# Wave attention: low parts of x on VectorE, sine tables from one rounded angle per phase, projection products ordered by part

## The reference, cut to what matters

```
qkvg = x @ Wqkvg.T + bqkvg                 # 256 -> 1024 channels
q_feat, k_feat = elu(q) + 1, elu(k) + 1
deposit = k_feat * v
alpha, omega, phi = softplus(wave_damping), wave_frequency, wave_phase
kernels = exp(-alpha * t) * cos(omega * t + phi)      # t = 0 .. 511, 16 heads
kernels /= sum(abs(kernels))
convolved = causal convolution of deposit with kernels (512 places)
field_c = softmax(field_coupling) @ convolved         # over heads
out = (q_feat * field_c * sigmoid(gate)) @ Wout.T + bout
x = layernorm(x + out)
```

## Time and profile before

| | |
|---|---|
| time, median of 3 | 1128.72 us |
| profiled execution, first to last instruction | 1136.1 us |
| PE busy | 1029.5 us (91%) |
| DVE busy | 792.9 us (70%) |
| ACT busy | 461.3 us (41%) |
| POOL busy | 467.0 us (41%) |
| wave attention | about the first 173 us of the span |

### The profile page before, as it was taken

The page is one execution under the profiler, slowest core; times in us unless marked ns, Lnnn a source line. Parts: engine busy times, 40 slices in busy tenths (PEclk is TensorE's granted clock), DMA queues, the critical chain, the costliest instruction groups (busy, mean ns, idle before and its releaser), DMA issues.

```text
span 1136.1 us, 19209 instructions
## 1 busy us (share of the span) xinstructions
PE 1029.5 (91%) x5944; PEld 898.8 (79%) x5945; DVE 792.9 (70%) x1338; ACT 461.3 (41%) x782; POOL 467.0 (41%) x455
## 2 busy tenths in 40 slices
PE   4879974669999999999999999998999999999994
PEld 3657753559999999899997788787888888888883
DVE  7978989699999998678878634333444444446886
ACT  5835434324444444556773122222222223233336
POOL 3211113224554444622210288886650400008886
PEclk9989987679999999999999999999999999999997
DMA  7100020000000000031133155756333111213435
GB/s 291 38 19 19 0 84 0 33 1 1 1 0 0 0 0 2 1 117 50 44 127 115 49 193 174 237 166 208 106 106 110 49 53 51 69 49 112 125 107 185
DMA packets 41349, 87.80 MB, mean 77 GB/s; under 512 B 5971, under 2 KB 27733, under 8 KB 39893
## 3 DMA queue, kind: packets, MB, share of 16 engines
q0 software_dynamic: 9696, 35.66, 10.2%
q1 hardware_dynamic: 20804, 39.20, 9.6%
q10 hardware_dynamic: 10800, 12.32, 3.5%
HBM read 57.80 MB, written 29.36 MB: 77 GB/s over the span
## 4 chain that ended last, share of the span: by engine, by line
PE 55%; DVE 14%; DVEq 9%; POOL 8%; issue 8%; ACT 3%; DMA 1%; POOLq 1%; another core or an unknown queue 0%; ACTq 0%
PE PS L1736 15%; PE PS L1738 14%; PE PS L1737 14%; POOL gathered L994 6%; PE PS L2108 3%; PE PS L1860 3%; DVEq L1320 2%; DVEq L1216 2%; POOL pause L998 1%; DVEq L1332 1%; DVE hx L1228 1%; PE PS L2092 1%; PE PS L1765 1%; DVEq L1229 1%; DVE qinv L1219 1%
## 5 line engine op out<-in xcount | busy, mean ns | idle before, releaser
L1673 DVE TENSOR_TENSOR hb<-PS,gs 128x512 f32<-128x512 f32 x71 | 49.1, 692 | 150.2 <-ACT gs L725 145.1
L994 POOL DMA_INDIRECT gathered<-expert_outputs,pos x64 | 66.5, 1040 | 139.3 <-DMA expert_outputs<-ye 127.1
L1736 PE MATMUL PS<-EWs,xeh 128*128 x284 | 118.8, 418 | 0.0
L1738 PE MATMUL PS<-EWs,xel 128*128 x284 | 111.5, 392 | 0.0
L1737 PE MATMUL PS<-EWs,xeh 128*128 x284 | 110.9, 391 | 0.0
L725 ACT ACTIVATE gs<-PS 128x512 f32<-128x512 f32 x71 | 42.6, 600 | 158.4 <-PE PS L1738 143.9
L1736 PE MATMUL PS<-WGh,bxh 128*128 128x352 f32 x256 | 88.5, 346 | 14.1 <-DVE hv L1314 12.1
L1860 PE MATMUL PS<-WD,htf 128*128 128x256 f32 x384 | 88.5, 380 | 1.6 <-ACT htf L522 1.5
L1677 DVE TENSOR_TENSOR hel<-PS,heh 128x512 fp32r<-128x512 f32 x71 | 49.1, 692 | 55.2 <-ACT heh L730 48.0
L1736 PE MATMUL PS<-EWs,heh 128*128 x284 | 85.7, 302 | 2.1 <-issue 1.1
L1737 PE MATMUL PS<-WGl,bxh 128*128 128x352 f32 x256 | 85.8, 335 | 0.0
(11 more groups left out here) (364 smaller groups left out, 3081.0 us busy)
## 6 DMA issues: line engine op xcount, KB each, us to landing
raw_of<-experts POOLq DMA_DIRECT2D x6, 1536.0 KB
expert_outputs<-ye SPq DMA_DIRECT2D x71, 128.0 KB
xe<-tokens_by_expert ACTq DMA_DIRECT2D x65, 128.0 KB
xraw<-xT SPq DMA_DIRECT2D x8, 512.0 KB, 5.0
X<-x SPq DMA_DIRECT2D x1, 4096.0 KB, 16.9
tokens<-X SPq DMA_DIRECT2D x8, 512.0 KB, 3.2
y<-X SPq DMA_DIRECT2D x7, 512.0 KB
raw_of<-experts SPq DMA_DIRECT2D x2, 1536.0 KB, 9.7
```

What stands on the lines that cost most here:

```text
L994: pool.indirect_dma_start(out=gathered[c][:, j, t], out_offset=None, in_=YS, in_offset=bass.IndirectOffsetOnAxis(ap=pos[:, j, 4 * c + t:4 ...
L1673: dve.tensor_tensor(hb[:, h], PS[:, 3], gs[:, h], ALU.mult).then_inc(e_hb, 1)
L1736: pe.matmul(out_, wh, vh, start=first, stop=False)
L1738: return pe.matmul(out_, wl, vh, start=False, stop=last_)
```

## The change

Three things are done.

**Low parts of x.** All eight `split_low` leave POOL and are done on DVE. The places are: piece 0 and 1 in the start (the second after the angles), piece 2 after `half(0,0,0)`, piece 3 after `conv(0)`, and in batches 1 and 2 the next batch's first piece after `half(b, par, 0)` and its second after `conv(b)`. In the start, the weights' low parts (`weight_low`) come first of all on DVE.

**Angles.** The product by omega's rest is no longer reduced by itself; it is added to the reduced one in the same instruction. Each phase is rounded once, with no quarter turn, in place of once for each of four tables. ACT takes the sine of the angle, and for the cosine the absolute value of the angle first and then the sine of a quarter turn less that: 4 Abs and 8 Sin in place of 8 Sin.

**Projection.** The six matmuls of a bank are ordered by part: two high by high, two with `WQl`, two with `xl`. PE starts at `wq_hi` and `x_hi`, and waits for `wq_lo` and `x_lo` only before the first matmul that reads them.

Two and then four matmuls now stand ahead of the waits for the low parts. The diff, cut to its core:

```diff
@@ scalar
-            for i, (table, turns) in enumerate(TABLES):
+            for i, (cos_, sin_, turns, phase) in enumerate(TABLES):
                 act.wait_ge(turns_done, i + 1)
                 for m in range(KD):
-                    act.activation(table[:, m], turns[:, m], ACT.Sin, bias=sm[:, PHASE[i], m:m + 1], scale=-TWO_PI).then_inc(act_s, 1)
+                    act.activation(cos_[:, m], turns[:, m], ACT.Abs, bias=sm[:, phase, m:m + 1], scale=-TWO_PI)
+                for m in range(KD):
+                    act.activation(sin_[:, m], turns[:, m], ACT.Sin, bias=sm[:, phase, m:m + 1], scale=-TWO_PI).then_inc(act_s, 1)
+                act.drain()
+                for m in range(KD):
+                    act.activation(cos_[:, m], cos_[:, m], ACT.Sin, bias=sm[:, 14, m:m + 1], scale=-1.0).then_inc(act_s, 1)
@@ gpsimd
-                pool.tensor_tensor(xl[:, h], xraw[:, h], xh[:, h].bitcast(F32), ALU.subtract).then_inc(x_lo, 1)
@@ vector
+            def split_low(b, h):
+                dve.wait_ge(x_hi, 2 * b + h + 1)
+                dve.tensor_tensor(xl[:, h], xraw[:, h], xh[:, h].bitcast(F32), ALU.subtract).then_inc(x_lo, 1)
...
+            for m in range(KD):
+                dve.scalar_tensor_tensor(Wv[:, 0, m, 0:CH], iota, sm[:, 5, m:m + 1], F1[:, m], ALU.mult, ALU.add)
+            dve.drain()
+            dve.tensor_scalar(F2[:], Wv[:, 0, :, 0:CH], ROUND, None, ALU.add)
+            for m in range(KD):
+                dve.tensor_scalar(S2[:, m], Wv[:, 0, m, 0:CH], sm[:, 17, m:m + 1], ROUND, ALU.add, ALU.add)
+            dve.drain()
+            for turns in (F2, S2):
                 dve.scalar_tensor_tensor(turns[:, 0:KD], turns[:, 0:KD], ROUND, Wv[:, 0, :, 0:CH], ALU.subtract, ALU.subtract).then_inc(turns_done, 1)
+            split_low(0, 1)
...
             half(0, 0, 0)
+            split_low(1, 0)
...
             def batch(b, par, before):
                 half(b, par, 0)
+                if b < B - 1:
+                    split_low(b + 1, 0)
                 wave(b - 1, before)
...
                 conv(b)
+                if b < B - 1:
+                    split_low(b + 1, 1)
             conv(0)
+            split_low(1, 1)
@@ tensor, project(b, h)
-                pe.wait_ge(x_lo, c + 1)
+                pe.wait_ge(x_hi, c + 1)
...
+                        pe.matmul(PS[:, j], WQh[:, k, cols], xh[:, h, k], start=k == 0, stop=False)
+                    for k in range(KD):
+                        if j == ORDER[0][0] and c == 0:
+                            pe.wait_ge(wq_lo, k + 1)
+                        pe.matmul(PS[:, j], WQl[:, k, cols], xh[:, h, k], start=False, stop=False)
+                    if j == ORDER[h][0]:
+                        pe.wait_ge(x_lo, c + 1)
+                    for k in range(KD):
+                        mm = pe.matmul(PS[:, j], WQh[:, k, cols], xl[:, h, k], start=False, stop=k == KD - 1)
                     mm.then_inc(proj, 1)
-            pe.wait_ge(wq_lo, KD)
+            pe.wait_ge(wq_hi, KD)
             project(0, 0)
```

More of the change, by code:

```diff
@@ L206, in build @@
         assert place["at"] <= kept + EARLY_AT
-        (c_ld, c_whi, c_wlo, c_wp, c_whi2, c_wlo2, c_xt, c_xhi, c_xlo, c_y, c_yhi, c_ylo, c_z, c_zhi, c_zlo, c_sim, c_max,
+        (c_ld, c_whi, c_wlo, c_wp, c_xt, c_xhi, c_xlo, c_y, c_yhi, c_ylo, c_z, c_zhi, c_zlo, c_sim, c_max,
          c_exp, c_pt, c_phi, c_plo, c_pv, c_res, c_bias, c_mv, c_rs, c_ln) = (sem("c_" + n) for n in (
-            "ld", "whi", "wlo", "wp", "whi2", "wlo2", "xt", "xhi", "xlo", "y", "yhi", "ylo", "z", "zhi", "zlo", "sim", "max",
+            "ld", "whi", "wlo", "wp", "xt", "xhi", "xlo", "y", "yhi", "ylo", "z", "zhi", "zlo", "sim", "max",
             "exp", "pt", "phi", "plo", "pv", "res", "bias", "mv", "rs", "ln"))
@@ L314, in down_parts @@
             return 2 * AHEAD + 5 * (c - AHEAD) + (j + 1 if j < 3 else 5)
-        PHASE = (11, 20, 21, 23)
-        TABLES = tuple(zip((cosA, sinA, cosB, sinB), (F1, F2, S1, S2)))
+        TABLES = ((cosA, sinA, F2, 15), (cosB, sinB, S2, 16))
         block = ctx.enter_context(nc.Block())
@@ L569, in fold_high @@
                     act.wait_ge(c_wp, j + 1)
-                    act.activation(QKh[:, j].rearrange("p k c -> p (k c)"), PS[:, 2 + j], ACT.Copy, scale=(SCALE, 1.0)[j]).then_inc(c_whi2, 1)
+                    act.activation(QKh[:, j].rearrange("p k c -> p (k c)"), PS[:, 2 + j], ACT.Copy, scale=(SCALE, 1.0)[j]).then_inc(c_whi, 1)
             def x_high(c, h):
@@ L773, in _ @@
             pool.memset(zrow[:], 0.0)
-            def split_low(b, h):
-                pool.wait_ge(x_hi, 2 * b + h + 1)
-                pool.tensor_tensor(xl[:, h], xraw[:, h], xh[:, h].bitcast(F32), ALU.subtract).then_inc(x_lo, 1)
-            split_low(0, 0)
-            split_low(0, 1)
             pool.wait_ge(ld_c, 16)
@@ L800, in inverse_deviation @@
                 pool.tensor_tensor(nmr[:], nmr[:], rstd[:], ALU.mult).then_inc(rs_done, 1)
-            split_low(1, 0)
             for m in range(KD):
@@ L805, in _ @@
                 pool.tensor_tensor(Wv[:, 0, m, 0:CH], Wv[:, 0, m, 0:CH], cosB[:, m], ALU.mult).then_inc(kernel_set, 1)
-            split_low(1, 1)
             with pool.Fori(1, B - 1) as b:
-                for h in range(2):
-                    split_low(b + 1, h)
                 inverse_deviation(b - 1)
@@ L1028, in _, with weight_low @@
         def _(dve):
-            dve.wait_ge(ld_cp, 16)
-            dve.tensor_reduce(cs[:, 0], cpl[:], AX.X, ALU.max, negate=True).then_inc(dve_s, 1)
+            def split_low(b, h):
+                dve.wait_ge(x_hi, 2 * b + h + 1)
+                dve.tensor_tensor(xl[:, h], xraw[:, h], xh[:, h].bitcast(F32), ALU.subtract).then_inc(x_lo, 1)
+            def weight_low(k):
+                dve.wait_ge(wq_hi, k + 1)
+                dve.tensor_tensor(WQl[:, k], wraw[:, k], WQh[:, k].bitcast(F32), ALU.subtract).then_inc(wq_lo, 1)
+            weight_low(0)
             dve.wait_ge(ld_wc, 32)
@@ L1035, in _ @@
             dve.tensor_scalar(nbc[:], bc[:, 6:8], 0.5, None, ALU.mult)
-            dve.memset(sm[:, 14], 0.25)
-            dve.memset(sm[:, 15], 0.0)
+            weight_low(1)
             dve.drain()
@@ L1040, in _ @@
             dve.tensor_scalar(sm[:, 13], sm[:, 7], ROUND, ROUND, ALU.add, ALU.subtract)
+            split_low(0, 0)
+            dve.wait_ge(ld_cp, 16)
+            dve.tensor_reduce(cs[:, 0], cpl[:], AX.X, ALU.max, negate=True).then_inc(dve_s, 1)
+            dve.memset(sm[:, 14], TWO_PI / 4)
+            dve.memset(sm[:, 15], 0.0)
             dve.drain()
@@ L1043, in _ @@
             dve.tensor_tensor(sm[:, 17], sm[:, 7], sm[:, 13], ALU.subtract)
[L1044 to L1054, removed]
             dve.wait_ge(ld_c, 16)
@@ L1059, in _ @@
                 dve.tensor_scalar(F1[:, m], iota, sm[:, 4, m:m + 1], None, ALU.mult)
-                dve.tensor_scalar(F2[:, m], iota, sm[:, 5, m:m + 1], None, ALU.mult)
             dve.drain()
             dve.tensor_scalar(S1[:], F1[:], ROUND, ROUND, ALU.add, ALU.subtract)
-            dve.tensor_scalar(S2[:], F2[:], ROUND, ROUND, ALU.add, ALU.subtract)
+            dve.tensor_scalar(sm[:, 16], sm[:, 17], TWO_PI, None, ALU.mult)
             dve.drain()
             dve.tensor_tensor(F1[:], F1[:], S1[:], ALU.subtract)
-            dve.tensor_tensor(F2[:], F2[:], S2[:], ALU.subtract)
+            dve.wait_ge(act_s, 2)
+            dve.reciprocal(cs[:, 2], cs[:, 1]).then_inc(dve_s, 1)
             dve.drain()
-            dve.tensor_tensor(Wv[:, 0, :, 0:CH], F1[:], F2[:], ALU.add)
+            for m in range(KD):
+                dve.scalar_tensor_tensor(Wv[:, 0, m, 0:CH], iota, sm[:, 5, m:m + 1], F1[:, m], ALU.mult, ALU.add)
             dve.drain()
[L1070 to L1073, removed]
+            dve.tensor_scalar(F2[:], Wv[:, 0, :, 0:CH], ROUND, None, ALU.add)
[3 more added lines that the diff above has]
+            for turns in (F2, S2):
                 dve.scalar_tensor_tensor(turns[:, 0:KD], turns[:, 0:KD], ROUND, Wv[:, 0, :, 0:CH], ALU.subtract, ALU.subtract).then_inc(turns_done, 1)
+            split_low(0, 1)
             dve.wait_ge(ld_wo, 32)
@@ L1367, in fold_low @@
                 for j in range(2):
-                    dve.wait_ge(c_whi2, j + 1)
+                    dve.wait_ge(c_whi, j + 2)
                     dve.scalar_tensor_tensor(QKl[:, j].rearrange("p k c -> p (k c)"), PS[:, 2 + j], (SCALE, 1.0)[j],
-                                             QKh[:, j].rearrange("p k c -> p (k c)").bitcast(F32), ALU.mult, ALU.subtract).then_inc(c_wlo2, 1)
+                                             QKh[:, j].rearrange("p k c -> p (k c)").bitcast(F32), ALU.mult, ALU.subtract).then_inc(c_wlo, 1)
             step_pair = step
@@ L1741, in project @@
                 c = 2 * b + h
-                pe.wait_ge(x_lo, c + 1)
+                pe.wait_ge(x_hi, c + 1)
                 for j in ORDER[h]:
                     o = COLUMN[j]
```

(7 more changed lines are left out.)

## The result

The changed kernel takes 1118.0 us (median of 4 runs, 1116.4 to 1120.9) against 1129.2 for the kernel before: ratio 0.991, 95% interval 0.9891 to 0.9929. The forecast was 1119.6 us, 9.1 us less than before. Timed again later, when both kernels took about 10 us longer (1128.0 against 1138.6 us), the ratio is 0.9905 (0.9888 to 0.9921).

What follows compares the result with a forecast made beforehand. The bound changes hands: low parts to 13 us, ACT and DVE to about 64, PE to about 148, then DVE. 2.8 + 4.2 + 2.1 = 9.1 us less gave 1119.6 us; range 1116.3 to 1124.3.

Steps and rivals of the forecast that it cites:

- Holds in conv(0): conv(0) on DVE: two small operations held by POOL's pieces drop from 2.29 and 2.24 to about 0.16 us; 4.2 us won.
- The wait of project(3,0): Batch 2: residual(1) on DVE comes 3.6 us earlier, so PE's 2.09 us wait in project(3,0) goes; 2.1 us won.
- Rival (b): couple(0): TensorE at full clock after shorter idle, 3.4 instead of 5.9 us; 11.5 us less in all, 1117.2; chance 0.11.
- Start and tables: Start to features of piece 1: PE 4.2 us earlier, four activations cost 2.8, vanished kf wait returns 1.36; 2.8 us earlier.
- The clock in the start: Start: PE's first matmuls take 0.43 us each at the lower clock, 1.2 GHz; 1.5 us allowed if it lasts longer.
- couple(0) stays slow: couple(0) at 57 us: over 5 us of PE idle remains before it, so it still takes near 5.9 us.
- Rival (a): Start: PE's early start doesn't count, so the four added activations are a loss; 4.9 us less, 1123.8; chance 0.13.
- (c): POOL and DVE: moving work between them doesn't pay, holds go but as much returns; 2.8 us less, 1125.9; chance 0.05.
- (d): DVE: long rows aren't POOL's doing, a subtraction costs 2.25 us anywhere; 6.4 us more, 1135.1; chance 0.04.

Runs made afterwards that it cites:

- the run with thrown-away matmuls: Changed kernel plus 5 and 8 matmuls of constants, results unused, in PE's idle before couple(0) and couple(3); 1125.8 us, ratio to before 0.988.

## Why the prediction was right, and where it was not

The forecast was 9.1 us less. The medians differ by 11.2 us, the ratio 0.991 makes 10.2, and the traces 10.1 (10.8 between the second profiles).

- **Holds in conv(0), 4.2 us.** Right in mechanism and size: 2.13 and 2.10 us, gone and brought back at will.
- **The wait of project(3,0), 2.1 us.** Right; PE came through that project 2.4 us faster. With the clock fallen behind the wait, as in the second profile above, it is 4.0. Rival (b) took the 0.47 us of the earlier trace rows for slow matmuls; but in the first profile, from which that row comes, the matmuls behind the wait start 0.23 us apart. DVE had time for the two pieces in batch 2: it still idled 0.8 us before `qf`.
- **Start and tables, 2.8 us.** The size was near (2.4 at the features of piece 1), and the terms are found in the changed kernel's trace: the early start of PE gives 3.9 us for 4.2, the tables take 9.3 for 9.1, the wait for `kf` is gone. But the gain doesn't hang on them. The low parts alone, with project(0,0) ending 0.65 us earlier in place of 3.9, reach the same place 0.4 us later: 0.65 us from the start and the 1.36 us wait for `kf`, which goes because DVE's angles are no longer held. The prediction had that wait go by the shorter angles, which are enough too (with the low parts on POOL, `kf` is done at 26.8 us). So the size of this term says little about its cause, and that it came out so near was in part luck. Early start, shorter angles and longer tables cancel each other to within 0.4 us in the trace; in time they can't be told from nothing (0.9904 against 0.991 and 0.9905), and with the low parts on POOL neither (0.9995).
- **The clock in the start.** The prediction reads 0.43 us per matmul as the lower level. The clock column of that row prints 1.00, so no row shows the granted clock there. With the tables undone, matmuls of this shape start 0.43 us apart at a granted clock of 0.50 (29.3 to 32.6 us), which bears the reading out.
- **couple(0) stays slow.** Right in kind (5.4 us), with 0.5 us less than the earlier trace rows at this place and again at couple(3): terms that I held at nothing. The range had room for them. The second is no effect of the change: the kernel before profiled again takes 5.43 us in couple(3), the changed one 5.51. The first may be one, since it is 4.80 us to the next project in both profiles of the changed kernel and 5.29 and 5.65 in those before, but 6.07 with the tables undone; it is not shown.
- **Rival (a)**, 4.9 us less, fell: the piece's DMA was in time. **Rival (b)** fell: with 4.9 us of idle before it the clock still fell. Its price for a full clock was near: a couple took 3.6 us in the run with thrown-away matmuls. **Rivals (c) and (d)** fell on the 1.22 us rows and on the run with the low parts back on POOL. The rule of the Trainium skill (Perfetto Trace Analysis, optimizing Scalar/DVE operations), that moving work between the two might not help, is no more than a warning, and here it helped: the work cost DVE 1.2 us where it waited anyway, and had cost 2.1 where it did not.
- **A new wait.** I named none for project(1,0), and 4.1 us appeared there in place of 3.2 in three waits, hidden behind `Y`.

## What to carry to other kernels

When a tiny VectorE instruction takes microseconds, look at what GpSimd runs at that moment. A piece of side work there may cost less on the busy engine itself, if it is put where that engine waits. Undo every part of a change one at a time: here one of three parts was the whole gain, and the other two about cancelled each other. A difference between two profiles is only the change's up to the first place where the untouched code runs at another pace.

## What was not expected of the hardware

The expert stage took 353 to 355 us or 364 to 368 us with the same instructions. It was long in the first profile of the kernel before and in all three profiles of the last timing, and short in the other nine, four of them on a chip that the record numbers as that of the last timing. The cause stays open. After an idle of 4.9 and 4.3 us TensorE's granted clock over couple(0) was 0.65 of full in the two profiles of the changed kernel (57.7 to 62.6 us), and after 5.5 us it was 0.50, that is 1.2 GHz, with the tables undone (57.4 to 62.4 us); without thrown-away matmuls the way to the next project took 4.7 to 6.1 us in kernels that differ nowhere near it. After the same idle of 2.1 us in project(3,0) the clock stayed at 1.00 in one profile of the kernel before and fell to 0.50 in the other. That alone spreads such comparisons by more than 1 us.
